# First loads on other queues, two merge groups regrouped by batch, one product of zeros fewer

## What is computed

```python
# layer 0, conditioning: LoRA expert of each batch (ids of 8)
hidden = relu(x @ wi.T + 2 * lora_in(x))      # common rank 16 + expert rank 16
y      = hidden @ wo.T + 2 * lora_out(hidden)
# layer 0, mixture of 4 experts, 4 rounds, top 2 by a gate
for r in range(4):
    w   = softmax(top2(cur @ Wg[r] + bg[r]))
    cur = cur + sum_e w[e] * (gelu(cur @ W1[e] + b1[e]) @ W2[e] + b2[e])
x = x + cur
# layer 1: language LoRA + embedding of each batch (ids of 4), then a gated net
h = silu(z @ w1 * s1) * (z @ w2 * s2)
h = gelu(h @ h1 * ..); h = gelu(h @ h2 * ..)
x = x + (h @ w3) * s3
```

## Time and profile before

| what | value |
|---|---|
| three runs | 480.96, 481.57, 481.77 us; median 481.57 |
| the profiled execution | 480.82 us, its span 479.0 us |
| TensorE busy | 474.5 us, 99% of the span |
| weight loads / VectorE / ScalarE / GpSimd busy | 82% / 81% / 82% / 25% |
| granted TensorE clock | 1.00 of full speed in every stretch |
| merge matmuls (L562, L565) | two passes each |
| DMA | 27.03 MB, 56 GB/s over the span; in the first 20 us 253 GB/s, the DMA engines 0.86 busy |

### The profile page before, as it was taken

One profiled execution on the slowest core, in us unless ns is written; L12 is line 12 of the kernel. 1 busy time (PEld: TensorE's weight loads), 2 busy tenths in 40 slices (PEclk: granted clock), 3 DMA queues, 4 the chain that ended last, 5 costly groups with the idle time before them and its releaser, 6 DMA issues.

```text
span 479.0 us, 7437 instructions
## 1 busy us (share of the span) xinstructions
PE 474.5 (99%) x2260; PEld 395.0 (82%) x2260; DVE 388.0 (81%) x638; ACT 393.6 (82%) x543; POOL 121.7 (25%) x102
## 2 busy tenths in 40 slices
PE   9999999999999999999999999999999999999997
PEld 8998888888888888888888888888888888888886
DVE  5898999999989898988889898889897758654343
ACT  4889888888889898888888798898888888697643
POOL 4995212121211212122212121171313144500000
PEclk9999999999999999999999999999999999999999
DMA  8603702021120202020202112120202000000001
GB/s 236 191 24 134 285 0 91 2 88 42 48 88 0 88 0 88 0 88 0 88 1 88 45 43 88 44 90 0 88 2 88 2 0 0 1 1 0 0 23 69
DMA packets 8299, 27.03 MB, mean 56 GB/s; under 512 B 2258, under 2 KB 3602, under 8 KB 6098
## 3 DMA queue, kind: packets, MB, share of 16 engines
q1 hardware_dynamic: 7090, 22.45, 13.4%
q0 software_dynamic: 288, 2.88, 1.7%
q10 hardware_dynamic: 896, 1.38, 1.0%
HBM read 25.26 MB, written 1.44 MB: 56 GB/s over the span
## 4 chain that ended last, share of the span: by engine, by line
PE 96%; POOL 2%; DMA 1%; DVE 0%; SPq 0%; issue 0%; ACT 0%; DVEq 0%
PE bank L538 34%; PE bank L541 34%; PE bank L544 26%; POOL ffn_lo L442 1%; PE bank L638 1%; PE bank L639 1%; DMA stage<-lora_all 1%; PE bank L565 0%; PE bank L562 0%; POOL xlo L447 0%; DVE stage L1076 0%; DVE prod L1076 0%; ACT ffn_hi L842 0%; DVE x L1312 0%; SPq L251 0%
## 5 line engine op out<-in xcount | busy, mean ns | idle before, releaser
L859 ACT ACTIVATE act_out<-bank,vec 128x512 f32<-128x512 f32 x256 | 164.9, 681 | 40.5 <-PE bank L544 28.7
L1154 DVE TENSOR_TENSOR hid_lo<-act_out,hid_hi 128x1024 fp32r<-128x1024 f32 x128 | 158.5, 1258 | 31.6 <-ACT hid_hi L864 31.5
L864 ACT ACTIVATE hid_hi<-act_out 128x1024 fp32r<-128x1024 f32 x128 | 135.9, 1062 | 8.3 <-ACT act_out L859 0.4
L502 POOL TENSOR_TENSOR cur<-cur,prod 128x512 f32<-128x512 f32 x48 | 64.8, 1350 | 233.5 <-DVE prod L1165 233.1
L538 PE MATMUL bank<-hid_hi,moe_hi 128*128 128x512 f32 x256 | 99.8, 390 | 0.0
L544 PE MATMUL bank<-hid_hi,moe_lo 128*128 128x512 f32 x256 | 99.7, 390 | 0.0
L541 PE MATMUL bank<-hid_lo,moe_hi 128*128 128x512 f32 x256 | 99.7, 389 | 0.0
L538 PE MATMUL bank<-xhi,moe_hi 128*128 128x512 f32 x256 | 99.6, 389 | 0.0
L541 PE MATMUL bank<-xlo,moe_hi 128*128 128x512 f32 x256 | 99.6, 389 | 0.0
L544 PE MATMUL bank<-xhi,moe_lo 128*128 128x512 f32 x256 | 99.6, 389 | 0.0
L538 PEld LDWEIGHTS bank<-hid_hi,moe_hi 128*128 128x128 f32 x256 | 48.1, 188 | 11.1
(11 more groups left out here) (134 smaller groups left out, 570.6 us busy)
## 6 DMA issues: line engine op xcount, KB each, us to landing
cw_all<-cw_dram SPq DMA_DIRECT2D x16, 1024.0 KB, 4.7
stage<-ffn_w POOLq DMA_DIRECT2D x1, 2304.0 KB, 8.5
cw_all<-moe_w SPq DMA_DIRECT2D x4, 512.0 KB, 7.5
stage<-lora_all SPq DMA_DIRECT2D x5, 160.0 KB, 4.6
x<-x_t SPq DMA_DIRECT2D x3, 256.0 KB, 5.2
out_t<-x SPq DMA_DIRECT2D x3, 256.0 KB, 2.4
cur<-cond_base ACTq DMA_DIRECT2D x2, 256.0 KB, 3.4
stage<-ffn_w POOLq DMA_DIRECT2D x1, 512.0 KB, 3.9
```

The costliest lines, as they stand in the source:

```text
L502: pool.tensor_tensor(cur[:, c, :], cur[:, c, :], prod[:, s % 2, :], ALU.add).then_inc(add_done, 1)
L859: act.activation(act_out[:, f // 2, f % 2, :], bank[:, f, :], ACT.Gelu_apprx_tanh, bias=vec[:, V_B1 + e * FC + f:V_B1 + e * FC + f + 1]).t ...
L864: act.activation(hid_hi[:, s % 2, 2 * pr:2 * pr + 2, :], act_out[:, pr, :, :], ACT.Copy)\
L1154: dve.tensor_tensor(hid_lo[:, s % 2, 2 * pr:2 * pr + 2, :], act_out[:, pr, :, :], hid_hi[:, s % 2, 2 * pr:2 * pr + 2, :].bitcast(F32), ALU ...
```

## The change

Four edits:

- x's first chunk is issued by SyncE, right behind the ids; the vectors and the gate's bias are issued by ScalarE, behind the first half of the base weights.
- Merge group 2 was (2,0), (3,0) and group 3 was (2,1), (3,1). Now group 2 is (3,0), (3,1) and group 3 is (2,0), (2,1).
- The banks go with it: (2,0) from bank 5 to 6, (2,1) from 6 to 7, (3,0) stays in 4, (3,1) goes from 7 to 5.
- Three products of zeros instead of four between groups 1 and 2.

```diff
-                ((2, 0), (3, 0)),
-                ((2, 1), (3, 1)),
+                ((3, 0), (3, 1)),
+                ((2, 0), (2, 1)),
...
-MERGE_BANKS = (6, 7, 2, 3, 5, 4, 6, 7, 4, 6, 7, 4, 6, 7, 4, 6)
+MERGE_BANKS = (6, 7, 2, 3, 4, 5, 6, 7, 4, 6, 7, 4, 6, 7, 4, 6)
...
-WARM, KEEP_WARM = 10, 4
+WARM, KEEP_WARM = 10, 3
...
             sp.dma_start(ids[:], batch_ids).then_inc(ids_in, 16)
-            sp.dma_start(vec[:], vecs).then_inc(small_in, 16)
-            sp.dma_start(gbias[:], gate_bias.to_broadcast([SQ, ROUNDS * EXPERTS])).then_inc(small_in, 16)
+            x_load(sp, 0)
             sp.wait_ge(ids_in, 16)
...
             base_load(act, 0)
-            x_load(act, 0)
+            act.dma_start(vec[:], vecs).then_inc(small_in, 16)
+            act.dma_start(gbias[:], gate_bias.to_broadcast([SQ, ROUNDS * EXPERTS])).then_inc(small_in, 16)
```

## The result

| what | before | changed |
|---|---|---|
| median of 15 runs each, us | 481.1 (480.59 to 482.16) | 482.89 (481.42 to 483.4) |
| ratio | | 1.003, 95% interval 1.0023 to 1.0037 |
| the profiled execution, us | 480.82, span 479.0 | 481.42, span 479.6 |
| busy TensorE / loads / VectorE / ScalarE / GpSimd | 99 / 82 / 81 / 82 / 25% | 99 / 82 / 81 / 82 / 25% |
| granted TensorE clock | 1.00 | 1.00 |

The change is slower, by 0.3%: some 1.4 us (0.003 x 481), between 1.1 and 1.8. (The ratio isn't that of the two medians, which lie 1.79 apart, at the upper end of this.) The forecast was 481.5 and the range ended at 482.5, so both were wrong. A trace is one draw; here the draws differ by more than the effect.

A forecast was written before the change was run, and what follows sets the result against it. TensorE, 99% busy, was taken as bound by three close chains ahead of its product at 18.04 us. First loads -0.10, product of zeros, grouping and waits 0 each, from the runs' median 481.57, gave 481.5 us; range 480.9 to 482.5.

The forecast's parts named there:

- The first loads: SyncE and ScalarE swap issue times of their first factors, so the first merge comes 0.10 us earlier; later base weights cost 0.
- rival three: The first factors' landing doesn't move, set by the bytes ahead and not the issue: nothing changes, 481.6 us; chance 0.08.
- Rival one: Base weights land behind x's second chunk, 1.1 us later, delaying VectorE's chain: +0.74 us, 482.3; chance 0.27.
- 0.09 + 0.11 + 0.06 of slack: Slack absorbing delay: before the first output product (0.09), ahead of merge group 5 (0.11), ahead of the 18.04 product (0.06).
- the row at 18.04: TensorE product starting at 18.04 us; whatever moves it moves the end by as much; forecast to start at 17.94.
- one case that I left out of the range: One more SyncE transfer goes ahead of the base weights: 1.8 us late, 483.0 us; chance 0.05.
- the three chains: Chains through GpSimd's low parts, TensorE's own work and VectorE after the base weights, within 0.2 us of one another.
- The grouping: Merge groups 2 and 3 on TensorE, regrouped by batch, still overlap fully: cost 0, other bound +0.71 us.
- Rival two: No overlap between merge groups 2 and 3: hidden products at 10.13 instead of 9.42, +0.44 us, 482.0; chance 0.18.
- The product of zeros: One fewer on TensorE starts merge group 2 0.22 us earlier, but the bank gate holds group 3: worth 0.
- waits: Three TensorE waits (batch 2's wide product, first output product, merge group 4) change with the tables: each 0.

The follow-up runs named there:

- without either: The change with the base weights' wait moved to the last sum and batches 2 and 3's factors' wait to merge group 4, computation partly altered: 481.28 us, ratio 0.9999.

## Why the prediction was wrong

**The first loads** are the step that failed, in both halves.

- "I take it that they change places", -0.10. SyncE took ScalarE's place only in part: in this trace it went out at 2.86, since it now waits for the ids to land; in the six others with the moved loads at 2.68 to 2.82. ScalarE slipped by 0.25 in all seven, not by 0.14: its two small transfers take 0.45 each to issue, where x's chunk alone took 0.45, and all that follows starts behind them. The later factors were thus issued 0.11 behind the later ones of before, not level with them, and the first merge stood at 5.73 for 5.75. It is at 5.59 to 5.82 in the seven traces with the moved loads and at 5.61 to 5.94 in eleven with those of before: a gain of 0.1 can't be told from none. Worth 0 as far as can be seen, as rival three had it.
- "The second half of the base weights is issued at 4.74 instead of 4.60 and lands at 8.74 ... Cost 0." It was issued at 4.88, behind x's chunk at 4.84, and landed at 9.3 in that trace, and at 9.1 to 11.0 in the traces of the change's other runs. I had moved a landing by the shift of its issue. The lead of one queue over the other was 0.17 and the slip larger than that, so the order turned. Measured cost: 1.4 us (1.1 to 1.8), where I had 0. The later issue by itself explains at most 0.28 of it (4.88 for 4.60), as the end follows the third sum one for one; the rest is that the transfer takes longer more often. That the turned order is what makes it take longer is the likeliest reading, and argued: in all traces that have both transfers in these places the one issued first also landed first, but no run turned the order and nothing else.

**Rival one** was the right mechanism, with all its marks: VectorE idle until past 9 and released by the base weights, a gap on TensorE ahead of the first output product. Its arithmetic nearly holds within one trace: a third sum 0.69 later, less the 0.09 + 0.11 + 0.06 of slack, makes 0.43, and the row at 18.04 moved by 0.30, the last product by 0.35. By TensorE's last product the slack was 0.34 and not 0.26. What was too small was its price (+0.74, at most 1.8 late in one case that I left out of the range) and its chance, 0.27. Both came from taking the landings of the earlier trace rows, 4.0 us for the base weights and 4.9 for x's chunk, as fixed durations. The 4.0 was the shortest that the profiles caught (once more in the run with x held back); the same 256 KB took 4.0 to 6.2. The execution I read was 0.75 below the median of its own three runs, and I treated that as a plain offset without asking what varied. (Not this wait alone: the kernel before has the same median without it. But two of the three chains start with a transfer, and their slack is a few tenths.)

The Trainium skill ("DMA: Bandwidth & Descriptors", section "Queues, rings and completion order") has the engines go round robin between queues. The traces agree in that the two large transfers land one after the other, the one issued first ahead, in either order, in all fourteen traces that have them in these places: 0.7 to 1.6 us apart in thirteen, and 0.2 in that of the three products of zeros alone. As they were issued only 0.03 to 0.21 apart, the turns would have to be long ones; how long a packet is no run shows. The same page's section "Issuing engines are not separate DMA queues" says that starting transfers on several engines "will only save the time on the sequencer". The traces add that it matters which queue is ahead: the wait for the base weights stood for the first landing of the two before, and for the second in the change.

**The grouping.** "I take full overlap, cost 0" was wrong in mechanism and right in price as far as can be measured, which was luck. Batch 2's first pass starts 0.56 behind group 2's first pass in all seven traces of that order, whether the bank gate opened earlier or not: 8.05 to 8.61 (gate 8.32), 8.50 to 9.06 with no base wait (gate 7.21 + 1.29 = 8.50), 7.96 to 8.52 without either (gate 6.94 + 1.28 = 8.22). The two groups take 1.65 (8.05 to the hidden products at 9.70) against 1.15 of before. Rival two's full wait would have been 2.1. So passes do overtake one another, but batch 2 was held until (3,1) was half through. The Trainium skill ("TensorE: Matmul & The Clock Gate", section "The mechanism") states a strict order for matmuls; taken for the two passes of a float32 product, the rows disagree with it. It cost nothing measurable: groups alone 0.9998 (0.9985 to 1.0012), which leaves room for 0.6. In the change group 2 also starts earlier (8.05 for 8.27), so the hidden products are only 0.28 later, against slack of 0.11 + 0.06, and in this trace the third sum's delay covers what is left. Whether the 0.6 to 0.8 us that are left without the base weights' wait are the later factors or this longer stretch behind them wasn't tried apart.

**The product of zeros** cost 0 as said, within the noise: group 2 started at 8.05 as worked out, and the run of that part alone gave 1.0003 (0.9989 to 1.0016). The changed **waits** weren't tried by themselves; the run of groups and banks alone has them all, and no loss that shows.

## What to carry over

A landing time in a trace belongs to that execution and that order of issues. When an edit shifts a queue by a tenth of a us, compare the shift with that queue's lead over the other one; if the order can turn, price the later transfer with the landing that the other one had, and more. And when the profiled execution lies well below the median, as that of the change does, take a second trace before reading the loss from the first: the wait for the base weights was 0.99 in one and 2.03 in the other. To test such a cause, take the wait away in both kernels: the change alone shows a loss, the pair shows the door it comes through.

## What the runs showed of the hardware

- The same 256 KB, issued between 4.57 and 4.88, took between 4.0 and 6.2 us to land, in kernels with equal loads too (4.0 before; 6.0 with three products of zeros, whose loads are those of before). What makes this spread stays open.
- Even the order of the two queues isn't fixed by the program: in one kernel ScalarE was 0.21 ahead in one execution and 0.03 behind in another, on another chip.
- Two small transfers on ScalarE's queue took 0.45 us each to issue, the table load started behind them at 2.21 instead of 1.73, and the first factors went out 0.25 later, at 2.92 in all seven traces. SyncE, relieved of one, stood 0.4 to 0.6 for the ids and went out between 2.68 and 2.86, where it mostly did at 2.81.
- Holding 256 KB of x back left the base weights' landing at 4.0 in the one execution traced, no shorter.
- The stretch from TensorE's last product to the end of the run took 5.2 to 5.8 us in twenty traces of kernels that are the same there.
